# A scan stage on one core: ScalarE's side work laid evenly between the recurrence's steps, and transposed inputs written with four images side by side

## The reference, cut to what matters

```python
Wx = einsum('bti,hi->bth', ln(t), W); Wx = (Wx - mean) * rsqrt(var + eps) * gamma + beta
def step(yt, wx_t):                       # 3136 steps, one behind the other, for 64 images at once
    yt = sigmoid(wx_t + yt @ V.T)
    return (yt, yt)
...
# layer 1, for every token: three gates from ln(x), and h after 16 steps of the same linear map
x_n = ln(x); fg, ig, delta = gates(x_n @ W + b)
h = fg * (A h) + delta * ig * (B x_n)     # 16 times from h = 0, complex, written in closed form by squarings
x = x + h
```

## Time and profile before

| what | value |
|---|---|
| median of three runs | 14605.63 us |
| the profiled execution | 14537.58 us |
| its span | 14535.8 us |
| busy over the whole span: PE, DVE, ACT, POOL | 79%, 76%, 68%, 28% |
| attention, scan, experts | to about 5200, to about 11650, to 14535.8 us |

### The profile page before, as it was taken

The page is one execution under the profiler, slowest core; times in us unless marked ns, Lnnn a source line. Parts: engine busy times, 40 slices in busy tenths (PEclk is TensorE's granted clock), DMA queues, the critical chain, the costliest instruction groups (busy, mean ns, idle before and its releaser), DMA issues. The chain is left out here.

```text
span 14535.8 us, 248087 instructions
## 1 busy us (share of the span) xinstructions
PE 11419.5 (79%) x87538; PEld 8744.4 (60%) x87538; DVE 11053.6 (76%) x22880; ACT 9833.3 (68%) x22679; POOL 4012.8 (28%) x3975
## 2 busy tenths in 40 slices
PE   7888888888888867777777777777777547776998
PEld 5666666666666645555555555555555235555888
DVE  6777777777777718999999999999999965554133
ACT  6888888888888846666666666667666567776100
POOL 5444444445444421212111211112121111211000
PEclk9999999999999967777777777777777677777555
DMA  3333333333333321111111111111111133333599
GB/s 69 86 81 82 81 82 87 76 90 73 90 77 86 75 61 41 53 53 53 51 47 52 53 53 53 51 46 53 53 52 40 23 84 94 99 90 89 172 316 309
DMA packets 1967708, 1189.72 MB, mean 82 GB/s; under 512 B 48853, under 2 KB 1900056, under 8 KB 1958436
## 3 DMA queue, kind: packets, MB, share of 16 engines
q1 hardware_dynamic: 1554148, 967.87, 26.3%
q10 hardware_dynamic: 408832, 205.55, 5.0%
q0 software_dynamic: 3648, 2.20, 0.1%
HBM read 708.85 MB, written 466.62 MB: 81 GB/s over the span
## 5 line engine op out<-in xcount | busy, mean ns | idle before, releaser
L1236 PEld LDWEIGHTS s_pW<-s_XU,s_vh 128*128 128x128 f32 x6272 | 1415.7, 261 | 1969.1 <-ACT s_XU L1107 1699.7
L1236 PE MATMUL s_pW<-s_XU,s_vh 128*128 128x64 f32 x6272 | 1493.2, 331 | 1071.4 <-ACT s_XU L1107 1071.4
L1107 ACT ACTIVATE s_XU<-s_pW,s_zb 128x64 f32<-128x64 f32 x3136 | 995.7, 318 | 1788.7 <-PE s_pW L1236 1738.1
L1265 PE MATMUL s_pG<-s_wg,s_XNT 128*128 128x384 f32 (+1 forms) x3200 | 1506.0, 559 | 37.5 <-ACT s_Z L1086 37.5
L832 POOL TENSOR_TENSOR s_rst<-s_var,s_epst 128x16 f32<-128x16 f32 (+1 forms) x100 | 141.7, 1417 | 3906.6 <-DVE s_var L79 3906.6
L408 ACT ACTIVATE KB<-pV,qkb 32x392 f32<-32x392 f32 x2048 | 1190.5, 581 | 25.0 <-PE pV L498 1.1
L248 POOL TENSOR_TENSOR SS<-SS,mx 128x784 f32<-128x784 f32 x512 | 769.5, 1503 | 804.8 <-DVE mx L341 804.6
L1203 PEld LDWEIGHTS s_pY<-s_hident,s_XU 128*128 128x128 f32 (+1 forms) x3200 | 752.2, 305 | 177.7 <-issue 129.6
L1711 PE MATMUL c_pS<-c_OX,c_Wm 64*112 64x128 f32 x3584 | 737.6, 420 | 91.1 <-DVE c_X L1727 76.6
L460 ACT ACTIVATE XH<-XR,nm,rs 112x128 f32<-112x128 f32 x1792 | 733.6, 485 | 92.1 <-POOL nm L267 83.6
L506 PE MATMUL pS<-KB,QT 128*64 128x196 f32 x8192 | 793.7, 336 | 0.0
(11 more groups left out here) (249 smaller groups left out, 31958.3 us busy)
## 6 DMA issues: line engine op xcount, KB each, us to landing
XL<-in_x_dram SPq DMA_DIRECT2D x64, 1568.0 KB, 12.4
XR<-in_x_dram SPq DMA_DIRECT2D x64, 1568.0 KB, 18.0
x_dram<-XR SPq DMA_DIRECT2D x64, 1568.0 KB, 8.1
xh_dram<-XH SPq DMA_DIRECT2D x64, 1568.0 KB, 8.1
r_X<-x_dram SPq DMA_DIRECT2D x64, 1568.0 KB, 14.2
c_X<-x_dram SPq DMA_DIRECT2D x64, 1568.0 KB, 19.4
out_dram<-c_X ACTq DMA_DIRECT2D x64, 1568.0 KB, 13.9
s_XQ<-xh_dram ACTq DMA_DIRECT2D x384, 256.0 KB, 2.8
```

The lines of the kernel that those rows point to most:

```text
L1107: act.activation(XU[j % 2][:, t, :], pW[t // R % 2][:, B * (t % R):B * (t % R) + B], ACT.Tanh, bias=zb[:, 0:1], scale=0.5).then_inc(u_sb, 1)
L1236: pe.matmul(pW[t // R % 2][:, B * (t % R):B * (t % R) + B], vh[:], before, start=False, stop=True, skip_group_check=True).then_inc(z_ps, 1)
L1265: pe.matmul(pG[i % 3][0:tc, 0:3 * C], XNT[:, i, 0:tc], wg[:], start=True, stop=True).then_inc(g_ps, 1)
```

## The change

It writes the tables of steps anew and moves the waits along. On ScalarE, XN becomes two images a step for eight steps, from k = 7 (k = 11 in slot 0), and the squares stand at k = 6, 15, 17, 19, 21, 22, 24. The copies of inputs go to k = 1, 3, 5, 8. On TensorE, `turn_u` for the next tile goes to k = 17, 19, 21, 24, the inputs' transposes to k = 0, 2, 4, 7, and those of XN to every second step from k = 9 (13 in slot 0). The semaphore counts on VectorE follow the new order of the squares; VectorE's own order stays. Besides, the transposes of inputs write every fourth column of `pX`, so that a token's four images lie side by side, and the copy writes runs of four values in XU where it wrote single values 64 apart.

```diff
+        TURN_IN = (0, 2, 4, 7)
+        KEEP_IN = (1, 3, 5, 8)
+        TURN_U = (17, 19, 21, 24)
+        KEEP_U = (18, 20, 22, 25)
+        def normal_at(s):
+            return 11 if s == 0 else 7
...
-                    dve.wait_ge(am, o * NA + 3)
+                    dve.wait_ge(am, o * NA + 1)
                     did(dve.scalar_tensor_tensor(t1, d0, -2.0, t1, ALU.mult, ALU.subtract))
...
-                    dve.wait_ge(am, o * NA + 5)
+                    dve.wait_ge(am, o * NA + 3)
                     did(dve.scalar_tensor_tensor(t2, d1, 2.0, t2, ALU.mult, ALU.subtract))
...
+                    dve.wait_ge(am, o * NA + 4)
                     did(dve.scalar_tensor_tensor(f0[:, 0], f0[:, 0], -0.25, d0, ALU.add, ALU.add))
                     did(dve.scalar_tensor_tensor(t0, t0, 1.0, d0, ALU.add, ALU.mult))
-                    dve.wait_ge(am, o * NA + 6)
+                    dve.wait_ge(am, o * NA + 5)
...
-                act.copy(XU[n % 2][:, 0:size(n), b0:b0 + Q].rearrange("c t b -> c b t"),
-                         pX[:, 0:Q * size(n)].rearrange("c (b t) -> c b t", b=Q)).then_inc(xt_sb, 1)
+                act.copy(XU[n % 2][:, 0:size(n), b0:b0 + Q],
+                         pX[:, 0:Q * size(n)].rearrange("c (t b) -> c t b", b=Q)).then_inc(xt_sb, 1)
...
-                    if conv and 10 <= k < 10 + NQ:
-                        q = k - 10
-                        if q == 0:
+                    i = 2 * (k - normal_at(s))
+                    if conv and 0 <= i < OS:
+                        if i == 0:
...
-                        for i in range(Q * q, Q * q + Q):
+                        for i in (i, i + 1):
...
+                    if o is not None:
+                        if k == 6:
+                            needs(4)
+                            act.activation(t1, t0, ACT.Square).then_inc(am, 1)
+                        if k == 15:
+                            act.activation(d1, d0, ACT.Square).then_inc(am, 1)
+                        if k == 17:
+                            needs(8)
+                            act.activation(t2, t1, ACT.Square).then_inc(am, 1)
+                        if k == 19:
+                            act.activation(f0[:, 0], t0, ACT.Square, bias=cols[0:tm, 1:2]).then_inc(am, 1)
+                        if k == 21:
...
+                            act.activation(f1[:, 0], t1, ACT.Square, bias=cols[0:tm, 2:3]).then_inc(am, 1)
+                        if k == 22:
+                            act.wait_ge(am, o * NA + 2)
+                            act.activation(d2, d1, ACT.Square).then_inc(am, 1)
+                        if k == 24:
+                            needs(11)
+                            act.wait_ge(am, o * NA + 5)
+                            act.activation(t1, t2, ACT.Square, bias=cols[0:tm, 2:3]).then_inc(am, 1)
...
-                    w = pe.transpose(pX[:, tn * b:tn * b + tn], XQ[i % 2][0:tn, b, :], ident[0:tn, 0:tn])
+                    w = pe.transpose(pX[:, 0:Q * tn].rearrange("c (t b) -> c t b", b=Q)[:, :, b], XQ[i % 2][0:tn, b, :],
+                                     ident[0:tn, 0:tn])
...
-                    if conv and s + 1 < NO and k in (24, 26, 28, 30):
-                        turn_u(oc + 1, (k - 24) // 2)
+                    if conv and s + 1 < NO and k in TURN_U:
+                        turn_u(oc + 1, TURN_U.index(k))
```

More of the change, by code:

```diff
@@ L1110, in _ @@
                         residual(oc, k - 1)
[L1111 to L1114, removed]
-                    if conv and 10 <= k < 10 + NQ:
-                        q = k - 10
-                        if q == 0:
+                    if conv and s + 1 < NO and k in KEEP_U:
+                        residual(oc + 1, KEEP_U.index(k))
+                    if prep and k in KEEP_IN:
+                        keep_turned(j, s, KEEP_IN.index(k))
+                    i = 2 * (k - normal_at(s))
+                    if conv and 0 <= i < OS:
+                        if i == 0:
                             act.wait_ge(rs_d, oc + 1)
@@ L1121, in _ @@
                             wait(act, n_ps, oc * NQ)
-                        for i in range(Q * q, Q * q + Q):
+                        for i in (i, i + 1):
                             w = act.activation(XN[0:tc, i, :], X2[oc % NX][0:tc, i, :], ACT.Identity,
                                                bias=nmr[0:tc, i:i + 1], scale=rst[0:tc, i:i + 1])
[L1125 to L1139, removed]
+                        if i % Q == Q - 1:
+                            w.then_inc(xn_d, 1)
+                    if conv and k - normal_at(s) - 3 in (0, 2, 4, 6):
+                        q = (k - normal_at(s) - 3) // 2
                         act.wait_ge(n_ps, oc * NQ + q + 1)
@@ L1146, in _ @@
                                        ACT.Identity, bias=cols[:, 0:1]).then_inc(n_sb, 1)
[L1147 to L1157, removed]
+                    if o is not None:
[10 more added lines that the diff above has]
+                        if k == 21:
+                            if conv:
+                                act.wait_ge(bx_d, oc + 1)
+                            act.activation(f1[:, 0], t1, ACT.Square, bias=cols[0:tm, 2:3]).then_inc(am, 1)
[6 more added lines that the diff above has]
+                            act.activation(t1, t2, ACT.Square, bias=cols[0:tm, 2:3]).then_inc(am, 1)
+                    if scan and s == NO - 2 and k == 26:
+                        act.wait_ge(mag_d, j + 1)
+                        act.activation(sc_[0:size(j)], sa[0:size(j)], ACT.Tanh, scale=0.5).then_inc(th_d, 1)
                     if conv and k > K - OS:
@@ L1248, in _ @@
                         turn_u(oc, k)
-                    if conv and s + 1 < NO and k in (24, 26, 28, 30):
-                        turn_u(oc + 1, (k - 24) // 2)
[L1251 to L1254, removed]
+                    if conv and s + 1 < NO and k in TURN_U:
+                        turn_u(oc + 1, TURN_U.index(k))
+                    if prep and k in TURN_IN:
+                        turn_inputs(j, s, TURN_IN.index(k), oc)
+                    q = k - normal_at(s) - 2
+                    if conv and q in (0, 2, 4, 6):
+                        if q == 0:
                             if scan and s == NO - 2:
@@ L1258, in _ @@
                                 pe.wait_ge(xt_sb, ((j + 1) * NO + s) * NQ + NQ)
-                        turn_normal(oc, tc, k - 11)
+                        turn_normal(oc, tc, q // 2)
                     if conv and k >= K - OS:
```

## The result

The changed kernel takes **14,858.6 us** (median of 3 runs, 14,849.5 to 14,889.0) where the kernel before takes 14,605.6: ratio 1.0185, 95% interval 1.0147 to 1.0222. It is slower, as forecast (14,875 us), by 253 us. The profiled execution of the changed kernel took 14,889.0 us, its span is 14,887.2.

What follows compares the result with a forecast made beforehand. VectorE bounds the kernel: a chunk lasts 239.1 us plus VectorE's waits. 8.4 + 3.6 - 0.4 - 0.4 = +11.2 us a chunk, over 24 chunks +269 us, gives 14,875 us on the runs' median level; range 14,690 to 15,040.

Steps and rivals of the forecast that it cites:

- (a): XN in slot 0, eight gaps instead of four: VectorE's wait grows from 5.4 to 13.8 us, +8.4 a chunk.
- gap 17: Time from step 17's recurrence tanh to the next, with a turn_u: 5.8 us in slot 0, 3.4 in slots 1 and 2.
- does not come earlier: GpSimd's statistics result in slot 0, before XN: no earlier than before, since it hangs on VectorE.
- (b): Slots 1 and 2: three turn_u ahead of the last square make VectorE wait 3.8 us each; net +3.6 a chunk.
- gap 16: Time from step 16's recurrence tanh to the next, in slots 1 and 2: 0.9 us.
- (c): From the last square's sum to the next L991: VectorE needs 30.2 us, ScalarE some 25, standing about 5 at step 6.
- Rid of four turn_u: ScalarE's work from the last square's sum to the next L991 falls from 34.7 to some 25 us.
- (d): Input layout: each copy 0.35 us less, four a slot, worth 0 to 0.4 us a slot, taken as 0.
- larger loss: Rival: clock rises only at step 19 or 20, or strided transposes are slow; +18.8 us a chunk, 15,057 us; chance 0.14.
- faster: Rival: VectorE's late inputs are cured and nothing replaces them; -3.7 us a chunk, 14,517 us; chance 0.10.
- the right two points: L991 to the last square under 29.6 us; XN in slot 0 at 1.10 us a gap, 8.5 us in all.

Runs made afterwards that it cites:

- number 11: Number 3's kernel reordered: squares early, turn_u behind the last square, XN packed in slot 0 and spread elsewhere; 14,465.0 us, ratio 0.9898.
- number 5: Number 3's kernel with only turn_u moved early, to steps 17, 19, 21 and 24; 14,885.9 us, ratio 1.0197.
- number 2: The changed kernel with XN in slot 0 back in four gaps, at steps 10 to 13; 14,950.3 us, ratio 1.0247.
- number 3: The kernel before with the new input layout alone, all steps as before; 14,591.7 us, ratio 1.0004.
- number 8: The changed kernel with turn_u at 17, 26, 28 and 30, so only one early; 14,748.0 us, ratio 1.0124.
- numbers 9 and 10: Number 3's kernel with the first turn_u alone early, at step 17 or at 21, inputs at old steps; 14,590.7 and 14,653.9 us.
- number 12: Number 11's kernel with slot 0's statistics on VectorE ahead of L1000's product instead of behind it; 14,436.0 us, ratio 0.9890.

## Why the prediction was right, and where not

**The bound, right.** A chunk is VectorE's 239.1 us and what it waits: 238.8 + 22.1 after. Over the runs the rule gives the times within about 45 us: 24 × (244.6 − 249.2) = −110 us for number 11, measured −149; 24 × (261.7 − 249.2) = +300 for number 5, measured +288.

**(a) XN in slot 0: the size nearly right, as a price wrong.** Forecast a wait of 13.8 us, measured 12.1. The mis-sized term is gap 17: 5.8 forecast, 4.24 measured, XN 14.2 us instead of 15.9. The clock was low in only half of that gap (mean granted clock 0.75). GpSimd, "does not come earlier": right. But (a) charged the spread with +8.4 us, and number 2 shows that without the spread the same time is lost at the squares behind. Most of it belongs to turn_u, as (b) does.

**(b) The squares and turn_u, right.** Forecast 3.8 us at the last square in slots 1 and 2, measured 4.81 and 4.94; nothing in slots 0 and 3, measured 0.21 and none. Of the path in slot 1, the stretch from XN's first pair to the end of gap 15 was forecast 12.8 and took 12.2 us (7342.63 to 7354.79), gaps 16 to 23 were forecast 16.9 and took 18.4 (to 7373.18). The mis-sized terms are gap 16 (0.9 forecast, 1.66 measured) and gap 17 (3.4 and 4.25), which were priced at the high clock:

```profile
7354.79:7360.70 5.91, 5.91 (x19) 4.00 (x19) 5.91 (x4) 2.58 (x7) 0.00 (x0) 0.61 0.00 1
7360.70:7373.18 12.48, 11.56 (x47) 8.15 (x47) 9.03 (x7) 8.74 (x24) 0.00 (x0) 1.00 0.01 1
```

The granted clock was 0.61 in gaps 16 and 17 and 1.00 from gap 18 on. The old waits in slots 1 and 2 went.

**(c) The other arc, right, and more important than it was given.** Forecast "about 5 us" of standing at step 6, measured 5.47 in the row above and 405.9 / 64 = 6.3 on average. "Rid of four turn_u" counts one too many, since the one at step 24 still stands behind the last square; the last square's two later steps, which also leave this arc, make up for it. I used it only to say that a gain is capped. The runs show it to be the condition of the loss.

**(d) The layout, right in time, off in size.** Copy 575 ns for some 690 forecast, just under the 0.6 to 0.8 us given as a sign, and worth nothing (number 3). The rule quoted there from the Trainium skill (SBUF — State Buffer, Door 1: The DMA port swizzle), that non-contiguous PSUM access slows matmuls, is not borne out for these transposes: 370 ns in number 3 with strided writes, 371 before. The rival *larger loss*, which rested on it and on a clock that rises only at step 19 or 20, fell: in slots 0 and 1 of the chunk shown the clock is at 1.00 from gap 18 on. Its own sum is also a little off: two waits of 7 us less 4.0 are +10, not +9.

**Missed.** The inputs' transposes at 0, 2, 4, 7 were priced only as work. Their loads were not looked at. In the changed kernel the wait for them (83.3 us) lies ahead of the stand at step 6 and so costs nothing; in number 8 nothing stands behind it, and it costs time.

**The sum.** +11.2 us a chunk forecast, +12.0 by the rows, +11.6 by busy time. Against the medians +269 forecast and +253 measured. The rival *faster* set the right two points, and neither was reached: the arc from L1000's end to the last square's sum took 34.3 us (7340.31 to 7374.57), not under 29.6, and XN in slot 0 14.2 us, not 8.5. An order that meets the first of them exists (number 11).

## What to carry to other kernels

Where two engines pass work to each other twice in a round, look at both arcs. Work moved from one arc to the other is free until the engine that it is taken from begins to wait there; from then on each us moved is lost. Look for that wait in every slot: before XN in slot 0 ScalarE stood from the start, and there even one turn_u cost its time. So place what nobody waits for, here turn_u, behind the last result that the bounding engine needs, and not evenly. Undo parts in both directions (take one out, put one in alone): the parts here cost 390 us apart and 270 together, and the one that looked guilty in the profile, XN's 12 us, was not.

## What the runs showed of the hardware

Strided PSUM writes by fp32 transposes (every fourth column of 512) cost nothing: 370 ns a transpose against 371. Reading such a tile with ScalarE and writing runs of four values instead of single ones took the copy from 1031 to 572 ns.

A load of 256 KB for s_XQ took 8.3 us to be used in number 8, while the 16 DMA engines were busy for 99% of that stretch (SyncE's queue had issued a store and loads from 7322.57 on), against a median of 3.0 us from issue to landing in the same kernel. With the inputs at every third step (numbers 9 and 10) the transposes waited for it 1.8 and 3.3 us in the whole steady part.

A small GpSimd instruction ended just after the VectorE instruction beside it, and so took 0.69 or 1.78 us for the same 16 columns. The Trainium skill (SBUF — State Buffer, SBUF: two separate sides) says that VectorE instructions with two inputs in SBUF and GpSimd hold a shared pair of ports in turn, for a whole instruction. The two pairs of rows under number 12 agree with it.
